# Neighbourhood attention with mixture-of-experts FFN: engine order, copied key windows and one score product

## The reference

```python
qkv = ln(x) @ qkv_w.T + qkv_b            # 12 heads of 16
reg_kv = registers @ qkv_w[192:].T + qkv_b[192:]   # 16 register keys and values
scores = einsum('bnqe,bnke->bnqk', q, [k, reg_k]) / 4
scores = where(7x7 neighbourhood or register, scores, -1e30)
o = softmax(scores) @ [v, reg_v]
x = x + o @ out_w.T + out_b
t = x + moe(ln(x)) + shared_ffn(ln(x))   # 16 experts, top 2, inter 512; shared 1024
```

## Time and profile before

| | us |
|---|---|
| median of 3 runs | 1344.66 |
| lowest, highest | 1332.4, 1348.81 |
| profiled execution, device time | 1346.43 |
| its span, first to last instruction | 1344.6 |
| PE, DVE, ACT, POOL busy in the span | 1163.1, 503.9, 406.5, 391.5 |
| mean granted PE clock | 0.945 |

### The profile page before, as it was taken

One profiled execution on the slowest core, in us unless ns is written; L12 is line 12 of the kernel. 1 busy time (PEld: TensorE's weight loads), 2 busy tenths in 40 slices (PEclk: granted clock), 3 DMA queues, 4 the chain that ended last, 5 costly groups with the idle time before them and its releaser, 6 DMA issues. The chain is left out here.

```text
span 1344.6 us, 37382 instructions
## 1 busy us (share of the span) xinstructions
PE 1163.1 (86%) x14806; PEld 954.9 (71%) x14806; DVE 503.9 (37%) x1212; ACT 406.5 (30%) x949; POOL 391.5 (29%) x524
## 2 busy tenths in 40 slices
PE   3899787787787787768999999999999999999990
PEld 2566566666666666645677667679999999999880
DVE  3344555655655655546522212222222222222220
ACT  0244555555555555531111111112222222222110
POOL 3011011111111111100366620004555555555442
PEclk9899888998988998879999989999999999999995
DMA  2352422222222222221113222247888878888754
GB/s 64 120 169 89 117 92 86 79 88 84 81 88 88 78 87 87 79 63 30 30 34 88 70 84 82 78 143 203 213 226 223 219 219 222 214 221 221 199 133 120
DMA packets 111183, 165.18 MB, mean 123 GB/s; under 512 B 14984, under 2 KB 84312, under 8 KB 110824
## 3 DMA queue, kind: packets, MB, share of 16 engines
q1 hardware_dynamic: 91960, 142.68, 34.0%
q0 software_dynamic: 19056, 20.14, 9.2%
HBM read 130.91 MB, written 35.34 MB: 124 GB/s over the span
## 5 line engine op out<-in xcount | busy, mean ns | idle before, releaser
L565 POOL DMA_INDIRECT acc_dram<-ys,lists x87 | 137.6, 1582 | 296.7 <-DVE ys L957 135.1
L618 ACT ACTIVATE probs<-ps,nmax 128x212 f32<-128x212 f32 x432 | 152.9, 436 | 117.4 <-DVE nmax L750 117.4
L750 DVE TENSOR_REDUCE nmax<-ps 128x2 f32<-128x424 f32 x216 | 118.5, 590 | 139.6 <-PE ps L1063 139.2
L950 DVE TENSOR_TENSOR m_h<-m_sg,ps 128x512 f32<-128x512 f32 x87 | 59.8, 687 | 294.8 <-ACT m_sg L664 195.8
L1232 PE MATMUL ps<-xa,w13r 128*128 128x128 f32 x1392 | 169.8, 275 | 0.3 <-ACT xa L658 0.3
L1232 PEld LDWEIGHTS ps<-xa,w13r 128*128 128x128 f32 x1392 | 162.3, 192 | 0.5 <-issue 0.5
L1151 PE MATMUL ps<-c_x,sw13a_sb 64*128 64x384 f32 x768 | 148.6, 498 | 13.1 <-DMA c_x<-xt_dram 4.6
L1076 PE MATMUL ps<-ident_sb,probs 128*98 128x128 f32 x864 | 136.4, 309 | 11.3 <-issue 4.9
L1248 PE MATMUL ps<-w_sb,m_h 128*128 x696 | 136.4, 339 | 0.0
L1076 PEld LDWEIGHTS ps<-ident_sb,probs 128*98 128x98 f32 x864 | 106.6, 147 | 26.5 <-issue 20.2
L651 ACT ACTIVATE s_sg<-ps 128x384 f32<-128x384 f32 x96 | 47.1, 490 | 249.8 <-PE ps L1151 208.7
(11 more groups left out here) (121 smaller groups left out, 1420.4 us busy)
## 6 DMA issues: line engine op xcount, KB each, us to landing
w13r<-in_w13a SPq DMA_DIRECT2D x87, 512.0 KB
w13r<-in_w13b SPq DMA_DIRECT2D x87, 256.0 KB
vst<-v_dram SPq DMA_DIRECT2D x144, 147.0 KB
v_dram<-a_v SPq DMA_DIRECT2D x12, 576.0 KB, 3.3
w_sb<-in_w SPq DMA_DIRECT2D x8, 768.0 KB
xn_dram<-xn SPq DMA_DIRECT2D x36, 128.0 KB
a_x<-in_x SPq DMA_DIRECT2D x12, 288.0 KB, 3.9
x_p<-in_x SPq DMA_DIRECT2D x36, 96.0 KB
```

Of the source, the lines that this page charges most:

```text
L565: nc.gpsimd.indirect_dma_start(acc_dram, bass.IndirectOffsetOnAxis(ap=lists[:, j, 0:1], axis=0), ys[:, j % V8, :], None, compute_op=ALU.ad ...
L618: nc.scalar.activation(probs[:, batch % 2, r, :], ps[:, r, 0:NKEY], ACT.Exp, bias=nmax[:, batch % 2, r:r + 1]).then_inc(b_exp, 1)
L750: nc.vector.tensor_reduce(nmax[:, batch % 2, 2 * half:2 * half + 2], ps[:, 2 * half:2 * half + 2, 0:NKEY], AX.X, ALU.max, negate=True).the ...
L950: nc.vector.tensor_tensor(m_h[:, j % 2, :], m_sg[:, j % 2, :], ps[:, 2 * (j % 2) + 1, :], ALU.mult).then_inc(d_h, 1)
```

## The change

A new buffer k_win holds, for three tiles, both halves and both key groups, a half's 196 window keys and the 16 register keys side by side. POOL copies the register keys once and the windows two tiles ahead. PE makes one product of 212 columns where there were two. The lists of all engines have another order and run over 11 further turns instead of 9; row_norm moves from DVE to POOL; the gate's logits move from bank 7 to bank 6, columns 384 to 399; the maxima are three reductions of 1, 1 and 2 banks; token_T, xT_out and gate come a tile later. Declarations of semaphores are left out:

```diff
+        k_win = place("k_win", [128, 3, 2, 2, NKEY], f32, at)
...
-            on_dve = batch + 1 - (batch + 1) // 3
+            on_dve = batch + 1 - (batch + 3) // 3
...
             for m in range(3, NT):
                 tile_in(m)
-                tile_out(m - 3)
-            for m in range(NT - 3, NT):
+                if m >= 4:
+                    tile_out(m - 4)
+            for m in range(NT - 4, NT):
                 tile_out(m)
...
+            def windows(m):
+                i, c = m // 3, m % 3
+                if m >= 3:
+                    pool.wait_ge(b_S, 24 * (m - 2))
+                for p in range(2):
+                    c0 = COL0[2 * c + p]
+                    for g in range(2):
+                        rows = k_T[:, g, i * BAND:i * BAND + KR * SIDE].rearrange("p (r c) -> p r c", c=SIDE)
+                        nc.gpsimd.tensor_copy(k_win[:, m % 3, p, g, 0:NWIN].rearrange("p (r c) -> p r c", c=WC),
+                                              rows[:, :, c0:c0 + WC]).then_inc(b_kwin, 1)
+            def row_norm(m):
+                c = m % 3
+                pool.wait_ge(b_pow, m + 1)
+                if m >= 3:
+                    pool.wait_ge(b_xn2st[c], 16 * (m // 3))
+                    pool.wait_ge(b_xTps, m - 2)
+                for lo, hi, at0 in ((0, D, 0), (128, D, D)):
+                    nc.gpsimd.tensor_scalar(xn2[:, c, at0:at0 + hi - lo], x2[:, c, lo:hi], b_mv[:, 0:1],
+                                            b_rs[:, 0:1], ALU.subtract, ALU.mult).then_inc(b_xn2, 1)
+            pool.wait_ge(r_k, 2)
+            for buf in range(3):
+                for p in range(2):
+                    nc.gpsimd.tensor_copy(k_win[:, buf, p, :, NWIN:NKEY], k_reg[:, :, :]).then_inc(b_kreg, 1)
+            pool.wait_ge(a_kev, NB)
+            pool.wait_ge(a_qev, 3 * NB)
+            windows(0)
+            windows(1)
+            stage_tile(0)
             for m in range(NT + 2):
-                if m < NT:
-                    stage_tile(m)
                 if m >= 2:
                     root(m - 2)
                 if 1 <= m <= NT:
                     normalize_o(m - 1)
+                if m >= 2:
+                    row_norm(m - 2)
+                if m + 2 < NT:
+                    windows(m + 2)
+                if m + 1 < NT:
+                    stage_tile(m + 1)
...
-                    act.wait_ge(b_nm, 2 * batch + r // 2 + 1)
+                    act.wait_ge(b_nm, 3 * batch + min(r, 2) + 1)
...
-            for turn in range(NBATCH + 9):
-                if turn % 3 == 2 and 0 <= turn // 3 - 2 < NT:
-                    xT_out(turn // 3 - 2)
+            for turn in range(NBATCH + 11):
                 if turn < NBATCH:
                     exps(turn)
                 if 1 <= turn <= NBATCH:
-                    if (turn - 1) % 3 == 2:
+                    if (turn - 1) % 3 == 0:
                         probsT_out(turn - 1, 0)
                     probsT_out(turn - 1, 1)
+                if turn % 3 == 2 and 0 <= turn // 3 - 3 < NT:
+                    xT_out(turn // 3 - 3)
...
-                for half in range(2):
-                    nc.vector.tensor_reduce(nmax[:, batch % 2, 2 * half:2 * half + 2],
-                                            ps[:, 2 * half:2 * half + 2, 0:NKEY], AX.X, ALU.max,
+                for lo, hi in ((0, 1), (1, 2), (2, 4)):
+                    nc.vector.tensor_reduce(nmax[:, batch % 2, lo:hi], ps[:, lo:hi, 0:NKEY], AX.X, ALU.max,
                                             negate=True).then_inc(b_nm, 1)
...
                 dve.wait_ge(b_V, 12 * m + 12)
+                if m >= 3:
+                    dve.wait_ge(b_gps, m - 2)
...
-            for turn in range(NBATCH + 9):
+            for turn in range(NBATCH + 11):
                 t, k = turn // 3, turn % 3
+                if 1 <= turn <= NBATCH and k != 1:
+                    probsT_out(turn - 1)
                 if k == 0 and 0 <= t - 2 < NT:
                     add_x(t - 2)
...
+                if k == 1:
+                    if 0 <= t - 2 < NT:
+                        row_stats(t - 2)
+                    if 0 <= t - 1 < NT:
+                        o_turn(t - 1)
+                    if 0 <= t - 4 < NT:
+                        logits_out(t - 4)
+                    if 0 <= t - 1 < NT:
+                        o_sums(t - 1)
                 if k == 2 and 0 <= t - 1 < NT:
                     o_back(t - 1)
                 if turn + 1 < NBATCH:
                     maxima(turn + 1)
...
+                if b == 0:
+                    pe.wait_ge(b_kwin, 4 * m + 4)
                 for r in range(4):
                     for p in range(2):
-                        c0 = COL0[2 * c + p]
-                        keys = k_T[32 * r:32 * r + 32, b // 2, i * BAND:i * BAND + KR * SIDE].rearrange(
-                            "p (r c) -> p r c", c=SIDE)[:, :, c0:c0 + WC]
-                        mm(out(r, p, 0, NWIN), query(r, p), keys, start=True, stop=False, skip_group_check=True)
-                for r in range(4):
-                    for p in range(2):
-                        mm(out(r, p, NWIN, NKEY), query(r, p), k_reg[32 * r:32 * r + 32, b // 2, :],
-                           start=False, stop=False, skip_group_check=True)
+                        mm(out(r, p, 0, NKEY), query(r, p), k_win[32 * r:32 * r + 32, m % 3, p, b // 2, :],
+                           start=True, stop=False, skip_group_check=True)
...
-            for turn in range(NBATCH + 9):
+            for turn in range(NBATCH + 11):
...
-                if k == 0 and 0 <= t - 3 < NT:
-                    gate(t - 3)
-                if k == 1 and 0 <= t - 2 < NT:
-                    token_T(t - 2)
+                if 1 <= turn <= NBATCH:
+                    values(turn - 1)
+                if k == 0:
+                    if 0 <= t - 3 < NT:
+                        token_T(t - 3)
+                    if 0 <= t - 4 < NT:
+                        gate(t - 4)
                 if k == 2 and 0 <= t - 1 < NT:
                     project(t - 1)
-                if 1 <= turn <= NBATCH:
-                    values(turn - 1)
```

More of the change, by code:

```diff
@@ L221, in metaformer_block @@
         b_S = sem("b_S")
+        b_kreg = sem("b_kreg")
+        b_kwin = sem("b_kwin")
         b_nm = sem("b_nm")
@@ L784, in add_x @@
                     dve.wait_ge(b_x2st[c], 16 * (m // 3))
+                    dve.wait_ge(b_xn2, 2 * (m - 2))
                 nc.vector.tensor_tensor(x2[:, c, :], ps[:, 7, 0:D], xb[:, c, :], ALU.add).then_inc(b_x2, 1)
@@ L788, in row_stats @@
                 dve.wait_ge(b_x2, m + 1)
+                if m:
+                    dve.wait_ge(b_xn2, 2 * m)
                 step(nc.vector.bn_stats(b_st[:, :], x2[:, m % 3, :]))
@@ L792, in row_stats @@
                 nc.vector.tensor_scalar(b_ve[:, :], b_mv[:, 1:2], 1e-5, None, ALU.add).then_inc(b_var, 1)
[L794 to L801, removed]
             def logits_out(m):
                 dve.wait_ge(b_gps, m + 1)
-                nc.vector.tensor_copy(logits[:, m, :], ps[:, 7, 0:E]).then_inc(b_lg, 1)
+                nc.vector.tensor_copy(logits[:, m, :], ps[:, 6, BAND:BAND + E]).then_inc(b_lg, 1)
             maxima(0)
             dve.wait_ge(s_wo, 2)
-            for turn in range(NBATCH + 9):
+            for turn in range(NBATCH + 11):
                 t, k = turn // 3, turn % 3
+                if 1 <= turn <= NBATCH and k != 1:
+                    probsT_out(turn - 1)
                 if k == 0 and 0 <= t - 2 < NT:
                     add_x(t - 2)
[L813 to L820, removed]
+                if k == 1:
[7 more added lines that the diff above has]
+                        o_sums(t - 1)
                 if k == 2 and 0 <= t - 1 < NT:
@@ L824, in _ @@
                     maxima(turn + 1)
-                if k == 0 and 0 <= t - 2 < NT:
-                    row_stats(t - 2)
-                if k == 1 and 0 <= t - 2 < NT:
-                    row_norm(t - 2)
             def wide(a):
@@ L1032, in _ @@
             pe.wait_ge(s_mq, 4)
+            pe.wait_ge(b_kreg, 6)
             def scores(batch):
@@ L1086, in values @@
                     pe.wait_ge(b_oraw, m)
+                    if m >= 4:
+                        pe.wait_ge(b_lg, m - 3)
                 on_dve, on_act = copies_by(batch)
@@ L1102, in project @@
                 pe.wait_ge(b_oT, 2 * m + 2)
-                if m:
-                    pe.wait_ge(b_xT, m)
+                if m >= 2:
+                    pe.wait_ge(b_xT, m - 1)
                 for a in range(2):
@@ L1111, in token_T @@
                 pe.wait_ge(b_xn2, 2 * m + 2)
-                pe.wait_ge(b_lg, m)
+                pe.wait_ge(b_x2, min(m + 2, NT))
+                if m:
+                    pe.wait_ge(b_xT, m)
                 for k in range(2):
@@ L1118, in gate @@
                 pe.wait_ge(b_xT, m + 1)
-                pe.wait_ge(b_x2, min(m + 2, NT))
+                if m:
+                    pe.wait_ge(b_lg, m)
```

(4 more changed lines are left out.)

## The result

The kernel after took 1229.0 us (median of 4 runs, 1212.8 to 1230.6), the kernel before, beside it, 1346.4 us (median of 4). The ratio is 0.909, 95% interval 0.900 to 0.918: faster. It lies a little under 1229.0 / 1346.4 = 0.913, because it leaves out the execution of 1230.6, which counts as slow, and takes in two further fast ones of the kernel after, 1211.5 and 1223.6 us. Direction and mechanism were forecast, 1245 us and a range of 1230 to 1288 were not far enough: the median lies 1 us under the range.

The account below looks back on a forecast made before the run. Bound: attention's chain of scores, maxima and exponentials plus a stall and slow clock. At 3.15 us a batch attention falls from 441.3 to 338.7 us; with +1.5 for start and end, 1346.4 - 101.1 gives 1245 us, range 1230 to 1288.

Parts of the forecast that it names:

- The ring: Attention batch chain: scores (PE), maxima (DVE), four exponentials (ACT), next scores; 3.18 us before, 3.05 forecast after.
- the two losses: In each attention tile: 1.88 us of ACT standing in xT_out ahead of the exponentials, 0.95 us mean from slow clock.
- the clock would come back by itself: PE's granted clock in attention: full outside the first tile once the stall goes, -0.95 us a tile.
- The price of the maxima: DVE's reductions as 1 + 1 + 2 banks: -0.07 us a batch, ends -0.23 and +0.10.
- the windows would be hidden: POOL's four window copies a tile, 0.45 us each: covered, with POOL busy 4.5 of 9.4 us.
- three ties with it: PE's work in two turns and DVE's o_turn wait for the gate nearly equal the chain: 0.10 us a batch added.
- the score product: One PE score product in place of two: -0.06 us a batch, ends 0 and -0.28.
- Start and end: Attention's edges: first scores wait for window 0, +0.5 us; drain with one more gate and POOL's norm, +1.0.
- The clock that still falls: PE clock in attention falls as before, one turn a tile stays slow: 10.3 us a tile, 1275 us; chance 0.13.
- the window copies as a bound: POOL's copies ahead of each tile's scores decide from 1.7 us a copy; 1372 us at 2.6; chance 0.06.
- the stall that only moves: Token transpose or ACT copy late again, 1.88 us stays: 11.3 us a tile, about 1310 us; chance 0.06.
- The ties cost more: o_turn's gate wait and PE's full turns cost 0.4 and twice 0.15 us more: 10.15 a tile, 1269 us; chance 0.12.

Follow-up runs that it names:

- The first experiment: Kernel before with only ACT's xT_out moved behind the exponentials and probability copies of its turn: 1263.3 us, ratio 0.942.
- The in-place run: Kernel after with window product on k_T read in place and register product apart, POOL's copies kept: 1234.7 us, ratio 0.923.

## Why the prediction fell short

*What was right.* The ring as the bound, the two losses on top of it, and that the clock would come back by itself. The run with two reductions shows the ring: its 0.09 us appear in full in the two turns that it bounds. The first experiment shows the two losses and the clock. The granted clock was 0.90 while PE was busy for 2.95 of the 5.06 us of a turn k=1, and 0.99 once that turn was 3.95. The clock was priced at 0.95 us a tile, and turn k=2 gave 0.86 there. The Trainium skill's TensorE: Matmul & The Clock Gate, Part 1, has activity release the throttle; these two clocks agree with it. The price of the maxima, -0.07 a clean ring by the third exponential (0.09 measured), was right too, and so was that the windows would be hidden: at three times the copies nothing moved. The Trainium skill's GPSIMD Engine Reference, section 4.1, has elementwise work on GpSimd about twice as slow as on VectorE with two inputs and roughly at line rate with one. The norm has one tensor input beside two scalars for each partition; the pair takes 1.60 us on POOL and took 0.72 on DVE (315.69). So here one input came out over twice as slow, which is not what the page has, and the measurement decides. My 0.8 for it was half of what it takes; covered as it is, that cost nothing.

*The step that failed* is "three ties with it (PE twice, DVE once) never cost nothing, I add 0.10: 3.15 a batch". Of the three, two cost nothing: k=0 and k=1 run at 2.99. Only k=2, with the projection, is PE's, and that one costs 0.11, so the mean is 0.04 and not 0.10. The ring itself is 2.99 and not 3.05, which is the other 0.06. Under both lies a term that was mis-sized, the score product, "-0.06 a batch": the ring got 0.10 shorter (0.97 for 1.07), and PE's issue of the scores, 0.75 us in my sums for PE, fell from 0.81 to 0.64. That relieved the very engine with which I had the ring tie. The in-place run gives the whole, 17.2 us or 0.16 a batch, against 0.06. A batch took 3.03 us in 104 of them (137.0 to 463.1 less 10.9 for the first tile), and (3.15 - 3.03) x 104 = 12 us are most of the 16 between 1245 and 1229. Against the profiled execution, 1212.8 us, the forecast was 33 us too high: 12.6 by S, 3.1 by start and end, 16.9 by the later stages.

*Start and end,* taken as +1.5, came to about -1.6. The first scores came 1.2 later, but without any window copy they came at 136.7, and with them anywhere from 135.7 to 138.7, so no copy need be seen in that. From the last scores to the shared FFN it was 21.2 us, 24.0 before: the last turn k=1 lies in this drain and lost its stall as well, which I had not counted. With xT_out moved in the kernel before it was 20.8 (506.0 to 526.8), which bears this out.

*The range.* For attention it was wide enough: its low end had 323 us where S is 326.1. It was missed by 1 us because start and end were 3.1 less than taken (with them the low end is 1227), and because it held the unchanged stages at the value of one execution, 743.5 us. They lie anywhere within 23 us over the traces of this study, and a low end that leaves this out is too high by itself, whatever the mechanism is worth. That 1229.0 came so close to the low end and not further under it is luck: the same kernel, run again, had 1211.1.

*The rivals.* The clock that still falls, the window copies as a bound and the stall that only moves are out, by the profile after and the runs above. "The ties cost more" had it the wrong way round. Two of the signs named ahead came out otherwise: the turns are 2.99, 2.99 and 3.10 us and not 3.1 to 3.2 in all three, and in k=1 the maxima do start right behind the reciprocals of o_sums, which was to be a sign of being wrong and cost nothing.

## What to carry to other kernels

Where several engines tie with the ring, price the edits by what they free on each engine and not by the ring alone: the merged product was worth 0.16 us a batch where it shortened the ring by 0.10, because it also took 0.17 us of issue from PE, which was next to bind. An in-order engine that stands in a side job ahead of the ring's next step holds up the ring, and the idle stretch can cost the clock of the turn behind it: moving one such job was 72 of 115 us, some 30 of them by the clock. Where the job goes, the next wait comes out: ACT's 1.88 us a tile were worth 1.17 in the kernel before, since PE's wait for the norm and a DVE busy for the whole turn lay right behind it. And before a range is drawn, the spread of the stages that are not touched belongs in it.

## What the hardware showed that was not expected

- A per-partition subtract and multiply with two scalar operands takes GpSimd 1.015 us for 192 elements and 0.582 for 64, while a plain copy of 196 in rows of 14 takes 0.31 us in sequence.
- Products from 14 rows of 14 with a pitch of 48 and from 196 dense columns cost PE the same here, S being 343.3 us either way.
- That the later stages run 720.6 to 743.6 us with unchanged code is open: the traces have the spread in all three of their parts (shared FFN 295 to 304 us, experts 400 to 412, the end 24 to 32), and no run was made to find its cause. Both traces of the kernel before, as it is and with xT_out moved, have 743.5 and 743.6, the ten others 720.6 to 739.5. So it is not excluded that the change shortens these stages by some us. The medians, each less that of the kernel before beside it and less what S explains, leave from -8 to +16 us for all that lies outside S, too wide to tell. In the kernel with the norm on DVE the best median of the study was seen, 1205.3 us, but its S is that of the kernel after, so it is not shown to be faster.
